# A selective-scan and ternary-FFN kernel: the input term of the scan made by TensorE for five of 16 pairs of states, and states handled in pairs

## The chip, the cores and the metric

One core of one Trainium2 chip runs the whole program. The metric is the device time of one launch in microseconds (us). The kernel before takes 226.84 us, the median of 3 runs (226.61 to 227.04). Engines are called by their names here: TensorE (PE in the profile), VectorE (DVE), ScalarE (ACT), GpSimd (POOL) and SyncE (SP), which issues nearly all the transfers.

## The reference, cut to what matters

Four sequences of 256 tokens, 256 channels. A state-space layer (16 states per channel) is gated by the normalised x and added to x; then comes a feed-forward block with ternary weights and 8-bit activations.

```python
x = x + ssm(ctx, layernorm(x))            # layer 1
x = x + ffn(layernorm(x))                 # layer 2

def ssm(h, z):                            # h (4,256,128), z (4,256,256)
    u = silu(depthwise_conv4(in_proj_w @ h) + conv_b)          # 256 channels x 256 steps
    dt_lo, B, C = split(x_proj_w @ u, [8, 16, 16])
    delta = softplus(dt_proj_w @ dt_lo + dt_proj_b)
    for t: state = state * exp(delta[t] * A) + delta[t]*u[t]*B[t]   # 16 states per channel
           y[t] = sum_n state[n] * C[t, n]
    return (y + D * u) * silu(z)

def bit_linear(x, w, b):                  # x in 127 steps of its token's maximum
    return round(x*127/gx)*gx/127 @ clip(round(w/gw), -1, 1)*gw + b
def ffn(x): return bit_linear(silu(bit_linear(x, gate)) * bit_linear(x, val), out)
```

## The kernel before, in words

**Tiling.** The four sequences go in two groups `g` of two (`BG`); channels lie on the 128 partitions in two halves `eh`. A row of work is 128 partitions x 512 (two sequences of 256 steps, one half of the channels, one state). So a group has 16 states x 2 halves = 32 units, and the kernel has 64 units in all, taken in order of the state, `eh` the inner loop.

**One unit of the scan.** ScalarE writes the decay exp(delta*A) into one of three PSUM banks (`decays`, line 653). GpSimd writes the drive, du*B, for both halves of one state at once, 128x1024, from `du` and from `b_wide`, the rows of B that a transfer has copied onto all partitions (`scan_drive`, lines 489 and 491). VectorE runs the scan (`scan`, line 898): one input is the decay in PSUM, the other the drive in SBUF. The state is then multiplied ("weighed") by C. For 22 of the 32 states VectorE does it, 128x512 each (line 908), with C spread over the partitions in the PSUM bank `cwide` by a TensorE product of a selector and C cut in three bf16 parts (`spread_c`, line 1177). For the ten states in `POOL_C` GpSimd does it, 128x1024 (line 501), with C loaded onto all partitions by a transfer. TensorE adds the weighed rows, transposed, into `ysum` (line 1156).

**What sets the order.** Nothing reorders instructions: each engine runs its own list, which the loops over the 64 units write out, and the engines wait for each other by semaphores. All other work is hung between the units by tables of unit numbers at the head of the file (`PE_Z`, `DVE_SPLIT`, `POOL_SOFTPLUS`, ...): group 1's convolution, projections and softplus, the rounding and turning of the ternary weights, and from unit 33 on the gate and the feed-forward block of group 0. Group 1's feed-forward block comes after the last unit, with nothing beside it.

**Around it.** VectorE makes the statistics of x before the first unit (line 816) and normalises x in eight steps beside the first units (line 825), it splits C (lines 865 to 871), ends the softplus (lines 877 to 889) and clips the ternary weights (line 945). GpSimd makes D*u (line 435), powers for the norms (line 443), group 1's softplus in part (lines 461 to 469), adds x (line 509), the parts of the token scales (lines 520 to 536) and adds the output bias to the residual (line 549).

Of the kernel before, what the change touches and what calls it, by code (L numbers as in the profile page):

```python
# [16 lines left out]
F32 = mybir.dt.float32  # L20
# [35 lines left out]
PE_Z, ACT_Z = (10, 11, 34, 36), (37, 38)  # L56
PE_PROJ, ACT_U, ACT_PROJ = 11, 14, 14
PE_PRE, ACT_PRE = (13, 14), (16, 18)
POOL_SOFTPLUS = (10, 11, 12, 13)
DVE_SPLIT, DVE_DELTA = 14, 27  # L60
ACT_WSUM, PE_WSUM, DVE_WSUM = (0, 2, 6), 11, 14
ACT_ROUND = (19, 21, 26)
PE_ROWS = (21, 26, 27, 28, 30, 31)
ACT_ROWS = (25, 28, 31, 32, 33, 35)
DVE_CLIP = (32, 34, 39)
DVE_GATED, DVE_STATS, DVE_INPUT = 33, 35, 37
POOL_SKIP, POOL_X1, POOL_RSTD, POOL_X1B = 9, 18, 19, 21
ACT_RND, POOL_PARTS = 40, 20
PE_COLS, ACT_COLS = 38, 41
PE_GATE, ACT_GATE = (39, 44, 51, 53), (44, 47, 56, 58)  # L70
PE_VAL, DVE_VAL, DVE_VAL2 = (45, 48, 59, 60), (46, 48, 60, 62), (47, 49, 61, 62)
ACT_QUANT, PE_TURN, ACT_TURN = (52, 54, 65, 68), (49, 54, 65), (53, 61, 67)
PE_OUT, DVE_OUT = (50, 58, 67), (51, 60)
POOL_C = (2, 5, 8, 13, 17, 19, 21, 24, 26, 28)
POOL_WAIT, SUM_WAIT = 3, 6
TURNS, WARM = (6, 6), (20, 3)


def on_pool(i):

    return i // EH in POOL_C


def rank(i):

    return sum(on_pool(k) == on_pool(i) for k in range(i))


def sums_at(j):

    return [i for i in range(max(0, j - SUM_WAIT), j)
            if 0 <= i < G * UNITS and j - (i - i % EH if on_pool(i) else i) == (SUM_WAIT if on_pool(i) else 2)]


SUMS = [i for j in range(G * UNITS + SUM_WAIT + 1) for i in sums_at(j)]


def work_tiles():

    first = ["inp", "ctx0", "conv0", "xin", "xproj", "dtw", "xc00", "conv1", "proj0", "pre00", "pre01", "ctx1"]
    scans = ["xc10", "xc11", "z0", "z1", "proj1", "wsum", "pre10", "pre11"]
    scans += [f"w{m}{k}" for m in "gvo" for k in range(4)] + ["z2", "z3"]
# [35 lines left out]
def block_program(nc, x, ctx, in_proj_w, conv_w, conv_b, x_proj_w, dt_proj_w, dt_proj_b, A_log, D,  # L142
# [3 lines left out]
    with stack:  # L146
# [6 lines left out]
        def sem(name):  # L153
# [59 lines left out]
        wrec = sb("wrec", [P, 4])  # L213
        ternary = sb("ternary", [P, 3, HT * DI], BF16)
# [7 lines left out]
        x1 = xhat[:, 0:GT]  # L222
        hn = xhat[:, GT:2 * GT]
# [18 lines left out]
        yflat = ysum[:].rearrange("p t e -> p (t e)")  # L242
        banks = [work[0][:], work[1][:], yflat[:, 0:BANK], yflat[:, BANK:2 * BANK],
                 *(d[:] for d in decay), cwide[:]]
        bc_rows = nc.dram_tensor("bc_rows", (G * 2 * NS, W), F32, kind="Internal").ap()
# [11 lines left out]
        s_ident, s_const = sem("ident_ready"), sem("constants_ready")  # L257
# [3 lines left out]
        s_xhat = sem("xhat_ready")  # L261
        s_cparts = sem("cparts_ready")
        s_expln = sem("exp_and_ln_ready")
        s_du = sem("du_ready")
        s_skip = sem("skip_ready")
        s_decay = sem("decay_ready")
        s_forget = sem("first_decays_zero")
        s_sel = sem("selector_ready")
        s_bstored = sem("b_and_c_rows_stored")
        s_cload = [sem(f"c_loaded{i}") for i in range(2)]  # L270
        s_poolw = sem("pool_wstate_ready")
# [1124 lines left out]
```

## Time and profile before

| | |
|---|---|
| median of 3 runs | 226.84 us (226.61 to 227.04) |
| span of the profiled execution | 224.8 us |
| what the median has over the span | 2.0 us |
| first unit's scan starts | 26.94 us |
| last weighing ends | 186.84 us |
| from there to the end | 37.96 us |
| VectorE busy over the span | 83% |
| PE, ScalarE, GpSimd busy | 67%, 58%, 61% |

The profiled execution is known by its span; the time of a run is what the table's first row gives, and the 2.0 us between them lie before the first and after the last instruction. The profile gives busy time per engine, groups of instructions by line, the instructions of an engine in order of time, and the chain of waits that ended last. A group of instructions is one line of the kernel; "out<-in" are the program's names of the tiles.

### The profile page before, as it was taken

Reading aid. Unit: us, or ns where it says so; the run is one execution under the profiler, and the core shown is the slowest. Engines: PE = TensorE matmul, PEld = TensorE weight load, DVE = VectorE, ACT = ScalarE, POOL = GpSimd, SP = SyncE. Lnnn points to the kernel's source line nnn. Section 1 sums busy time; section 2 is a strip of 40 time slices with the busy share of each in tenths; the row PEclk is TensorE's granted clock in tenths of the full one; section 3 lists DMA queues with packets and bytes.
Section 4 is the critical chain, followed back from the end, with each engine's and each line's share of the span. In section 5 each row is a group of like instructions: output and inputs, shape, how many; then the busy total and the mean of one; then the engine's idle time right before and its main releaser. Section 6 shows DMA issues by size and latency. Waiting matters only on the chain.

```text
span 224.8 us, 2405 instructions
## 1 busy us (share of the span) xinstructions
PE 150.9 (67%) x706; PEld 92.9 (41%) x706; DVE 186.5 (83%) x284; ACT 129.3 (58%) x197; POOL 136.8 (61%) x132
## 2 busy tenths in 40 slices
PE   6983088643979197059630777926986667899983
PEld 5531054232636186048620533504435265334552
DVE  3789999998089999999999968797869998838661
ACT  2578675336585996076341758736498015376772
POOL 5036499778900999896685999999139202691000
PEclk9995559978585769758785596985589969999999
DMA  4894943261400223004003304314000000000002
GB/s 107 231 343 123 339 146 112 87 189 42 140 13 0 75 66 92 4 0 141 0 0 98 135 3 136 73 71 140 23 1 3 23 0 0 0 28 0 23 23 70
DMA packets 12689, 17.44 MB, mean 78 GB/s; under 512 B 3468, under 2 KB 9012, under 8 KB 12678
## 3 DMA queue, kind: packets, MB, share of 16 engines
q1 hardware_dynamic: 12678, 17.30, 24.5%
q8 instruction: 5, 0.08, 0.2%
q14 instruction: 6, 0.05, 0.1%
HBM read 16.11 MB, written 1.19 MB: 77 GB/s over the span
## 4 chain that ended last, share of the span: by engine, by line
DVE 19%; PE 16%; ACT 9%; issue 6%; POOL 5%; DVEq 0%; POOLq 0%; ACTq 0%
DVE wstate L908 3%; PE work L1242 2%; DVE state L898 2%; PE work L1282 2%; DVE gam L981 2%; DVE xhat L825 2%; PE decay L1067 2%; ACT decay L653 2%; DVE pool_state L898 2%; DVE wstage L976 2%; POOL drive L491 2%; ACT gT L722 2%; ACT wstage L703 1%; PE decay L1242 1%; PE work L1249 1%
## 5 line engine op out<-in xcount | busy, mean ns | idle before, releaser
L491 POOL TENSOR_TENSOR drive<-du,b_wide 128x1024 f32<-128x1024 f32 x31 | 74.2, 2407 | 2.9 <-DVE state L898 1.8
L653 ACT ACTIVATE decay<-delta,aneg 128x510 f32<-128x510 f32 x64 | 42.9, 684 | 45.9 <-DVE state L898 23.3
L898 DVE TENSOR_TENSOR_SCAN state<-decay,drive 128x512 f32<-128x512 f32 x44 | 52.4, 1208 | 0.9 <-issue 0.9
L1156 PE MATMUL ysum<-ident,wstate 128*128 128x128 f32 x176 | 32.9, 332 | 10.6 <-DVE wstate L908 10.6
L908 DVE TENSOR_TENSOR wstate<-state,cwide 128x512 f32<-128x512 f32 x44 | 29.1, 663 | 12.2 <-issue 11.8
L1156 PEld LDWEIGHTS ysum<-ident,wstate 128*128 128x128 f32 x176 | 26.1, 172 | 18.8 <-DVE wstate L908 13.8
L501 POOL TENSOR_TENSOR pool_wstate<-pool_state,c_wide 128x1024 f32<-128x1024 f32 x10 | 23.7, 2367 | 11.4 <-PE ysum L1156 8.6
L898 DVE TENSOR_TENSOR_SCAN pool_state<-decay,drive 128x512 f32<-128x512 f32 x20 | 24.3, 1214 | 0.2 <-ACT decay L653 0.2
L1067 PE MATMUL work<-ident,wstage 128*128 128x128 f32 x80 | 14.2, 331 | 11.4 <-ACT ternary L677 7.7
L1177 PE MATMUL cwide<-cparts,sel 128*128 128x512 bf16 x22 | 10.6, 483 | 15.4 <-DVE wstate L908 14.2
L1067 PEld LDWEIGHTS work<-ident,wstage 128*128 128x128 f32 x80 | 11.8, 174 | 12.7 <-ACT ternary L677 8.1
L1242 PE MATMUL work<-ternary,qT 128*128 128x512 bf16 x46 | 16.3, 445 | 1.1 <-DVE wstage L976 0.8
L1156 PE MATMUL ysum<-ident,pool_wstate 128*128 128x128 f32 x80 | 13.3, 322 | 1.6 <-POOL pool_wstate L501 1.6
L716 ACT ACTIVATE wstage<-wstage,gam 128x512 f32<-128x512 f32 x16 | 10.6, 716 | 6.0 <-DVE gam L984 6.0
L509 POOL TENSOR_TENSOR xhat<-xhat,x_in 128x1024 f32<-128x1024 f32 (+1 forms) x2 | 3.6, 1814 | 16.0 <-DVE xhat L926 12.5
L1156 PEld LDWEIGHTS ysum<-ident,pool_wstate 128*128 128x128 f32 x80 | 11.9, 171 | 2.7 <-POOL pool_wstate L501 1.9
L976 DVE SCALAR_TENSOR_TENSOR wstage<-work,gam,wstage 128x512 f32<-128x512 f32 x12 | 8.7, 744 | 4.8 <-ACT wstage L703 3.4
L1067 PE MATMUL work<-ident,xhat 128*128 128x128 f32 x24 | 6.2, 420 | 9.6 <-ACT xhat L689 5.9
L1177 PEld LDWEIGHTS cwide<-cparts,sel 128*128 128x128 bf16 x22 | 2.5, 112 | 20.4 <-DVE wstate L908 17.6
L1156 PE MATMUL ysum<-ident,skip 128*128 128x128 f32 x16 | 3.0, 352 | 10.7 <-issue 8.7
L981 DVE TENSOR_REDUCE gam<-wstage 128x1 f32<-128x1024 f32 x8 | 9.8, 1220 | 0.3
L1249 PE MATMUL work<-bias_rows,acol 9*128 9x512 bf16 x23 | 9.8, 432 | 0.0
(180 smaller groups left out, 298.7 us busy)
## 6 DMA issues: line engine op xcount, KB each, us to landing
b_wide<-bc_rows SPq DMA_DIRECT2D x16, 512.0 KB, 4.5
c_wide<-bc_rows SPq DMA_DIRECT2D x10, 256.0 KB, 3.5
x_in<-in_x SPq DMA_DIRECT2D x2, 512.0 KB, 4.9
wstage<-in_L_ffn_gate_w SPq DMA_DIRECT2D x1, 1024.0 KB, 7.8
wstage<-in_L_ffn_val_w SPq DMA_DIRECT2D x1, 1024.0 KB, 10.3
wstage<-in_L_ffn_out_w SPq DMA_DIRECT2D x1, 1024.0 KB, 9.0
ctx_in<-in_ctx SPq DMA_DIRECT2D x2, 256.0 KB, 4.4
out<-wtap SPq DMA_DIRECT2D x4, 128.0 KB, 1.7
```

The lines of the kernel that those rows point to most:

```text
L491: nc.gpsimd.tensor_tensor(drive[:, m % NDR], du[:, m // NS], rows.unsqueeze(1).to_broadcast([P, EH, W]), ALU.mult).then_inc(s_drive, 1)
L501: nc.gpsimd.tensor_tensor(pool_wstate[:], pool_state[:, k % NPS], c_wide[:, k % 2].unsqueeze(1).to_broadcast([P, EH, W]), ALU.mult).then_i ...
L653: nc.scalar.activation(v[:, :, 1:L], d[:, :, 1:L], ACT.Exp, scale=aneg[:, eh, n:n + 1]).then_inc(s_decay, 1)
L898: nc.vector.tensor_tensor_scan(dst, decay[i % ND][:], drive[:, i // EH % NDR, i % EH], 0.0, ALU.mult, ALU.add).then_inc(s_scan, 1)
L908: nc.vector.tensor_tensor(wstate[:, rank(i) % NWS], state[:, rank(i) % NST], cwide[:], ALU.mult).then_inc(s_wst, 1)
L976: release(nc.vector.scalar_tensor_tensor(v, bank[:], gam[:, 3, t:t + 1], v, ALU.mult, ALU.mult), name)
L981: link(nc.vector.tensor_reduce(gam[:, 5, t:t + 1], gv[:, t], axis=AX.X, op=ALU.max, apply_absolute_value=True))
L1067: return nc.tensor.matmul(dst, lhsT=src, rhs=ident[0:src.shape[0], 0:src.shape[0]], start=True, stop=True, is_transpose=True, **flags)
L1156: last = nc.tensor.matmul(ysum[:, k, eh * P:(eh + 1) * P], lhsT=src[:, k * P:(k + 1) * P], rhs=ident[:], start=start and k % LB == 0, stop ...
L1177: nc.tensor.matmul(cwide[:], lhsT=sel[:, m % NS], rhs=cparts[:, m // NS], start=True, stop=True).then_inc(s_cwide, 1)
L1242: nc.tensor.matmul(bank[:], lhsT=qT[:, d, t * P:(t + 1) * P], rhs=wT[:, d, cols], start=d == 0, stop=False)
L1249: fill(nc.tensor.matmul(banks[TILE[name][0]], lhsT=acol[rows, t * P:(t + 1) * P], rhs=bias_rows[rows, cols], start=False, stop=True), name)
```

## The change

The loop goes over pairs of states. A slot is (pair of states, half of the channels, group): 32 slots, each 128x1024, of two units, one for each sequence. A scan is still 128x512, now one sequence with two states side by side.

- **Drive.** For five of the 16 pairs (`DIAG_PAIRS`; ten slots) GpSimd spreads B's columns on the diagonals of 128x128 matrices, one 128x1024 instruction a pair (`diagonals`), and TensorE multiplies the turned du by them into PSUM (`drives`, two products of 256 columns in float32 for a unit). For the other 11 pairs (22 slots) GpSimd multiplies du by B's rows on all partitions, 128x1024 (`drive_slot`), into `pool_drive` in SBUF.
- **Decay.** It lies in SBUF in place of PSUM, for all slots.
- **Weighing.** C is loaded onto all partitions for every pair; `cwide`, the selector and the split of C go. GpSimd weighs 22 slots (`weigh`), VectorE the ten in `DVE_SLOTS`, each in one 128x1024 instruction whose two inputs are both in SBUF.
- **Head.** dt_proj_w times x_proj_w's first rows is formed once (`wd`), so that the softplus doesn't wait for the projection; delta of the later halves is summed by TensorE (`add_delta`). The statistics of x move from ahead of the first unit to units 2 to 5. D*u becomes a TensorE product with a diagonal.
- **Others.** silu of the normalised x is one ScalarE instruction per tile (`silu_x`) in place of VectorE's normalising; the ternary weights come from ScalarE's Sign in place of copy and clip; VectorE adds x; two small instructions fewer per scale.

```diff
-NDR = 4
-ND = 3
-NPS = 2
-NB = 2
...
-POOL_C = (2, 5, 8, 13, 17, 19, 21, 24, 26, 28)
...
+ORDER = [(0, 0), (1, 0), (0, 1), (1, 1)] + [(p, eh) for p in range(2, NP) for eh in range(EH)]
...
+ND = 4
+NDRV = 4
+NST = 3
+NPW = 2
+NDG = 2
+NCW = 3
+NBW = 2
+NPD = 2
+DIAG_PAIRS = (0, 1, NP, NP + 2, NP + 4)
+DVE_SLOTS = (4, 6, 11, 13, 15, 17, 19, 21, 23, NSLOT - 1)
+POOL_LEAD = 2
...
-        decay = [pb(f"decay{i}", [P, BANK]) for i in range(ND)]
-        cwide = pb("cwide", [P, BANK])
+        decay = sb("decay", [P, ND, BG, 2, L])
+        pool_drive = sb("pool_drive", [P, NPD, BG, 2, L])
+        drive = [pb(f"drive{i}", [P, BANK]) for i in range(NDRV)]
...
+            def drive_slot(s):
+                g, p, eh = slot_parts(s)
+                k, r = g * NP + p, drive_rank(s)
+                w = wide_rank(k)
+                if r >= NPD:
+                    pool.wait_ge(s_scan, BG * [j for j in range(s) if not on_diag(j)][r - NPD] + BG)
...
+                rows = du[:, g, eh].rearrange("p (b l) -> p b l", b=BG).unsqueeze(2).to_broadcast([P, BG, 2, L])
+                nc.gpsimd.tensor_tensor(pool_drive[:, r % NPD], rows, b_wide[:, w % NBW], ALU.mult).then_inc(s_pdrive, 1)
...
+            for s in range(NSLOT):
+                for k in DIAG_PAIRS[2:]:
+                    if s == slots_of(k)[0] - DIAG_LEAD:
+                        diagonals(k)
+                if s + POOL_LEAD < NSLOT and not on_diag(s + POOL_LEAD):
+                    drive_slot(s + POOL_LEAD)
+                if s not in DVE_SLOTS:
+                    weigh(s)
+                if s == POOL_XRSTD:
+                    rstd(0)
...
             def scan(i):
-                nc.vector.tensor_tensor_scan(dst, decay[i % ND][:], drive[:, i // EH % NDR, i % EH], 0.0,
-                                             ALU.mult, ALU.add).then_inc(s_scan, 1)
+                s, b = divmod(i, BG)
...
+                if on_diag(s):
+                    dve.wait_ge(s_drive, BG * r + b + 1)
+                    rows = drive[(BG * r + b) % NDRV][:]
+                else:
+                    dve.wait_ge(s_pdrive, r + 1)
+                    rows = pool_drive[:, r % NPD, b].rearrange("p n l -> p (n l)")
+                if s >= NST and b == 0:
+                    wait_weighed(dve, s - NST)
+                nc.vector.tensor_tensor_scan(state[:, s % NST, b].rearrange("p n l -> p (n l)"),
+                                             decay[:, s % ND, b].rearrange("p n l -> p (n l)"), rows, 0.0,
+                                             ALU.mult, ALU.add).then_inc(s_scan, 1)
...
-                nc.vector.tensor_tensor(wstate[:, rank(i) % NWS], state[:, rank(i) % NST], cwide[:],
+                nc.vector.tensor_tensor(flat(wstate[:]), flat(state[:, s % NST]), flat(c_wide[:, k % NCW]),
                                         ALU.mult).then_inc(s_wst, 1)
...
+                for c in range(LB):
+                    t = b * LB + c
+                    last = nc.tensor.matmul(bank[:, :, c * P:(c + 1) * P], lhsT=duT[:, g, t, eh], rhs=bdiag[:, d % NDG, t],
+                                            start=True, stop=True)
```

On GpSimd, in the middle of group 0, the list before has a drive for every state (both halves) and here and there a weighing and a part of group 1's softplus:

```order
L491 TENSOR_TENSOR drive<-du,b_wide 128x1024
L461 TENSOR_SCALAR du<-mag 128x1024
L491 TENSOR_TENSOR drive<-du,b_wide 128x1024
L501 TENSOR_TENSOR pool_wstate<-pool_state,c_wide 128x1024
L465 TENSOR_SCALAR du<-du 128x1024
L491 TENSOR_TENSOR drive<-du,b_wide 128x1024
L467 TENSOR_TENSOR du<-du,mag 128x1024
```

After the change the same place of GpSimd's list (slots 2 to 8; 520 is the drive of the slot two ahead, 532 the weighing) is, following the power for x's norm:

```order
L483 TENSOR_SCALAR nv<-nv 128x8
L520 TENSOR_TENSOR pool_drive<-du,b_wide 128x1024
L532 TENSOR_TENSOR pool_wstate<-state,c_wide 128x1024
L520 TENSOR_TENSOR pool_drive<-du,b_wide 128x1024
L532 TENSOR_TENSOR pool_wstate<-state,c_wide 128x1024
L520 TENSOR_TENSOR pool_drive<-du,b_wide 128x1024 x2
L532 TENSOR_TENSOR pool_wstate<-state,c_wide 128x1024
L520 TENSOR_TENSOR pool_drive<-du,b_wide 128x1024 x2
```

The softplus has gone, and weighings stand between most of the drives; the power for the norm of x, which waits for VectorE's statistics, stands ahead of the first of these drives.

On VectorE, before, in the same part of group 0, scans (898) with a PSUM decay alternate with weighings of 512 (908):

```order
L898 SCALAR_TENSOR_TENSOR pool_state<-decay,drive 128x512
L908 TENSOR_TENSOR wstate<-state,cwide 128x512
L898 SCALAR_TENSOR_TENSOR pool_state<-decay,drive 128x512
L898 SCALAR_TENSOR_TENSOR state<-decay,drive 128x512 x2
L908 TENSOR_TENSOR wstate<-state,cwide 128x512
L898 SCALAR_TENSOR_TENSOR state<-decay,drive 128x512
L908 TENSOR_TENSOR wstate<-state,cwide 128x512
L935 TENSOR_SCALAR wgam<-work 128x3
```

After it, VectorE's list from the last statistics of x on, slots 3 to 6 (970 is the scan, `drive` in PSUM by TensorE, `pool_drive` in SBUF by GpSimd):

```order
L880 BN_STATS stats<-x_in 128x6 x2
L883 BN_AGGR mv<-stats 128x2 x2
L970 SCALAR_TENSOR_TENSOR state<-decay,drive 128x512 x2
L970 SCALAR_TENSOR_TENSOR state<-decay,pool_drive 128x512 x2
L983 TENSOR_TENSOR wstate<-state,c_wide 128x1024
L970 SCALAR_TENSOR_TENSOR state<-decay,pool_drive 128x512 x3
L1009 TENSOR_SCALAR wgam<-work 128x3
```

Most weighings have left VectorE's list, and from slot 4 on its scans read `pool_drive` and `decay`, both in SBUF.

## Rows read from the trace of the kernel before

**Rows 1.** The page's busy times: us, share of the span, instructions.

```profile
PE 150.9 (67%) x706; PEld 92.9 (41%) x706; DVE 186.5 (83%) x284; ACT 129.3 (58%) x197; POOL 136.8 (61%) x132
```

**Rows 2.** Three stretches: units of group 0, of group 1, the rest; busy us.

```profile
core 0: us, PE busy (x) PEld busy (x) DVE busy (x) ACT busy (x) POOL busy (x), PEclk, DMA share, GB/s
26.94:106.50 79.56, 51.57 (x230) 36.59 (x230) 71.52 (x80) 48.83 (x69) 61.69 (x29) 0.74 0.26 84
106.50:186.84 80.34, 51.27 (x241) 30.79 (x241) 70.34 (x100) 41.66 (x62) 54.10 (x40) 0.77 0.15 49
186.84:224.80 37.96, 31.97 (x185) 16.76 (x183) 24.02 (x57) 22.61 (x39) 11.07 (x37) 1.00 0.06 21
```

**Rows 3.** The page's groups: busy, mean ns of one, idle time before and its releaser.

```profile
L898 DVE TENSOR_TENSOR_SCAN state<-decay,drive 128x512 f32<-128x512 f32 x44 | 52.4, 1208 | 0.9 <-issue 0.9
L908 DVE TENSOR_TENSOR wstate<-state,cwide 128x512 f32<-128x512 f32 x44 | 29.1, 663 | 12.2 <-issue 11.8
L501 POOL TENSOR_TENSOR pool_wstate<-pool_state,c_wide 128x1024 f32<-128x1024 f32 x10 | 23.7, 2367 | 11.4 <-PE ysum L1156 8.6
```

**Rows 4.** Line 898's instructions: duration ns min/median/max.

```profile
L898 DVE TENSOR_TENSOR_SCAN state<-decay,drive x44: 1191/1210/1224, 26.9 to 184.4; 128x512 f32<-128x512 f32 x44
L898 DVE TENSOR_TENSOR_SCAN pool_state<-decay,drive x20: 1206/1216/1224, 37.8 to 167.9; 128x512 f32<-128x512 f32 x20
```

**Rows 5.** VectorE in order of time: start us, duration us.

```profile
21.41 0.69 DVE L882 TENSOR_TENSOR delta<-du,lnw 128x512 f32<-128x512 f32 x1
22.75 0.42 DVE L877 TENSOR_SCALAR du<-mag 128x512 f32<-128x512 f32 x1
23.93 1.65 DVE L880 TENSOR_TENSOR du<-pre,du 128x512 f32<-128x512 f32 x1
...
35.33 2.56 DVE L825 TENSOR_SCALAR xhat<-x_in,mv,nv 128x256 f32<-128x256 f32 x1
37.81 1.21 DVE L898 TENSOR_TENSOR_SCAN pool_state<-decay,drive 128x512 f32<-128x512 f32 x1
38.94 0.66 DVE L908 TENSOR_TENSOR wstate<-state,cwide 128x512 f32<-128x512 f32 x1
...
41.30 0.39 DVE L825 TENSOR_SCALAR xhat<-x_in,mv,nv 128x256 f32<-128x256 f32 x1
...
89.59 2.77 DVE L888 TENSOR_TENSOR delta<-du,lnw 128x1024 f32<-128x1024 f32 x1
92.47 3.17 DVE L889 TENSOR_TENSOR du<-delta,u 128x1024 f32<-128x1024 f32 x1
```

**Rows 6.** GpSimd in order of time, the same columns.

```profile
23.75 1.27 POOL L489 TENSOR_TENSOR drive<-du,b_wide 128x512 f32<-128x512 f32 x1 [3.05 <-DMA b_wide<-bc_rows]
28.33 9.41 POOL L491 TENSOR_TENSOR drive<-du,b_wide 128x1024 f32<-128x1024 f32 x4
...
88.94 5.62 POOL L491 TENSOR_TENSOR drive<-du,b_wide 128x1024 f32<-128x1024 f32 x2
95.72 2.34 POOL L491 TENSOR_TENSOR drive<-du,b_wide 128x1024 f32<-128x1024 f32 x1 [1.16 <-DVE du L889]
```

**Rows 7.** Groups with shapes kept apart, VectorE and GpSimd.

```profile
L816 DVE BATCH_NORM_STATS2 stats<-x_in 128x6 f32<-128x256 f32 x8 | 2.7, 410 | 0.0
L921 DVE TENSOR_TENSOR xhat<-ysum,szT 128x1024 f32<-128x1024 f32 x1 | 1.2, 1211 | 0.0
L418 POOL TENSOR_SCALAR_AFFINE_SELECT ident<-ident 128x128 f32<-128x128 f32 x1 | 0.3, 292 | 0.2 <-POOL ident L417 0.2
L443 POOL TENSOR_TENSOR nv<-nv,half 128x8 f32<-128x8 f32 x1 | 1.7, 1654 | 0.1
L549 POOL TENSOR_TENSOR x_in<-xhat,obias 128x256 f32<-128x256 f32 x4 | 2.8, 722 | 0.0
```

**Rows 8.** The page's transfers: KB each, median us from issue to landing.

```profile
b_wide<-bc_rows SPq DMA_DIRECT2D x16, 512.0 KB, 4.5
```

**Rows 9.** The chain of waits: start us, us, what.

```profile
123.10 0.52 POOL gam L520 x2
...
126.44 0.19 POOL apart L533
```

More of the change, by code:

```diff
@@ L89, in sums_at @@
[L89 to L95, printed above, removed]
+NP = NS // 2
+SLOTS = NP * EH
+UNITS = SLOTS * BG
+ORDER = [(0, 0), (1, 0), (0, 1), (1, 1)] + [(p, eh) for p in range(2, NP) for eh in range(EH)]
+NSLOT = G * SLOTS
+NUNIT = G * UNITS
+ND = 4
[5 more added lines that the diff above has]
+NBW = 2
@@ new lines, with slot_of, slot_parts, slots_of @@
+TURNS, WARM = (6, 6), (16, 3)
+def slot_of(g, p, eh):
+    return g * SLOTS + ORDER.index((p, eh))
+def slot_parts(s):
+    g, k = divmod(s, SLOTS)
+    p, eh = ORDER[k]
+    return g, p, eh
+def slots_of(k):
+    return sorted(slot_of(k // NP, k % NP, eh) for eh in range(EH))
+def pair_of(s):
+    g, p, _ = slot_parts(s)
+    return g * NP + p
+def on_diag(s):
+    return pair_of(s) in DIAG_PAIRS
+def drive_rank(s):
+    return sum(on_diag(k) == on_diag(s) for k in range(s))
+def wide_rank(k):
+    return sum(j not in DIAG_PAIRS for j in range(k))
@@ L237, in block_program @@
         work = [pb(f"work{i}", [P, BANK]) for i in range(2)]
[L238 to L239 removed]
         ysum = pb("ysum", [P, GT, DI])
[L242 to L245, printed above, removed]
+        drive = [pb(f"drive{i}", [P, BANK]) for i in range(NDRV)]
+        banks = [work[0][:], work[1][:], *(ysum[:, LB * b:LB * (b + 1)].rearrange("p t e -> p (t e)") for b in range(BG)),
+                 *(d[:] for d in drive)]
+        DRIVE0 = 4
+        bc_rows = nc.dram_tensor("bc_rows", (G, 2, NP, BG, 2, L), F32, kind="Internal").ap()
         bias_split = nc.dram_tensor("bias_split", (2, PARTS, HID), BF16, kind="Internal").ap()
@@ L762, in _ @@
+                if t == ACT_RND:
+                    for k in range(GT):
+                        ffn_round(0, k)
+                if t == ACT_COLS:
                     ffn_half(0, 0)
@@ new lines, in sums @@
+            def sums(s):
+                _, _, eh = slot_parts(s)
+                wait_weighed(pe, s)
+                src = wstate[:] if s in DVE_SLOTS else pool_wstate[:, pool_rank(s) % NPW]
+                for n in range(2):
+                    for t in range(GT):
+                        b, c = divmod(t, LB)
+                        last = nc.tensor.matmul(ysum[:, t, eh * P:(eh + 1) * P], lhsT=src[:, b, n, c * P:(c + 1) * P],
+                                                rhs=ident[:], start=False, stop=True, is_transpose=True,
+                                                skip_group_check=True)
+                last.then_inc(s_ysum, 1)
@@ L1340, in _ @@
                     ffn_products(0, PE_VAL.index(i), "val")
-            wait_weighed(pe, G * UNITS - 1)
+            for s in range((PE_OUT[-1] - SUM_LAG) // BG + 1, NSLOT):
+                sums(s)
             warm(WARM[0])
```

975 lines of the change are left out of this document (505 added, 470 removed).

## The prediction

> **What bounds the kernel now.** I read the busy times first [rows 1], then the same by stretches [rows 2], then the groups [rows 3], then VectorE and GpSimd side by side in order of time [rows 5, 6]. The reader is to see that VectorE is busy in 71.5 of 79.6 us of group 0's units and in 70.3 of 80.3 us of group 1's. The 64 scans and 44 weighings make 52.4 + 24.3 + 29.1 = 106 us of it (24.3 is 20 scans at the 1216 ns of [rows 4]). GpSimd is busy in 61.7 and 54.1 us of these stretches, so it has 44 us of slack. The rest, 37.96 us, is group 1's feed-forward block, which the change leaves nearly as it is.
>
> The second thing to see is that VectorE and GpSimd shut each other out. Line 889, 128x1024 with both inputs in SBUF, takes 3.17 us and line 888 2.77 us, where line 921, as large but with one input in PSUM, takes 1.21 [rows 5, 7]. Beside them GpSimd's two drives take 5.62 us, where four in a row take 9.41, 2.35 each [rows 6]: 0.9 us lost. The times fit turns: line 888 waits for the first drive, runs, the second drive runs while line 889 waits, and the next drive starts at 95.72, just after 889 ends at 95.64. Line 880 is the same on a small scale: it starts at 23.93 inside a GpSimd drive (23.75 to 25.02) and takes 1.65 us, where line 882, the same shape, takes 0.69 [rows 5, 6]. Line 825, SBUF to SBUF, takes 0.39 or 2.56 us [rows 5]. The scans never do this: 64 of them lie between 1191 and 1224 ns [rows 4], and each has its decay in PSUM.
>
> [...]
>
> **What the change does to that.** The scans of the 22 slots that GpSimd drives now read `decay` and `pool_drive`, both in SBUF. That is 44 of the 64 scans. The ten VectorE weighings also have two SBUF inputs. So I ask what must take turns from the first GpSimd drive on.
>
> *Head.* Before, the first scan starts at 26.94. The split of C and the statistics leave VectorE's path, TensorE gets more to do (the product of the two projections, turning B and du, summing delta, three drives), and all that ends, by my count of the same steps at about 0.7 us an operation of 512 [rows 5], near 25.7; bounds 24 and 28. Then come slots 0 to 3, driven from PSUM. VectorE runs six scans at 1.13 (from 37.81 to 38.94 in [rows 5]), one copy of 0.6 and the statistics of x (eight at 0.41 [rows 7] and eight small ones, 3.8 with the waits between them): 25.7 + 6.8 + 0.6 + 3.8 = 36.9. GpSimd stands at the power for x's norm until then, since it comes behind the weighing of slot 1; 1.65 us [rows 7] and three small ones make 2.5. Its first drive, slot 4's, starts near 39.4, and behind it wait slot 4's scan and the weighing of slot 2.
>
> *GpSimd from 39.4 on.* 22 drives at 2.35 = 51.7 [rows 6]. 20 weighings (22 less slots 0 and 1) at 2.35 (alone 2367 ns [rows 3]) = 47.0. Three diagonals: no row has this size; the nearest is line 418, 292 ns for 128 columns [rows 7], which by its slope would be about 1.05 for 1024, and the other bound is 2.35, a product of that size; I take 1.05, since it is the same operation: 3.2. A power 1.2, the scale parts 3.5 (123.10 to 126.63 [rows 9]), four additions at 0.72 = 2.9 [rows 7]. Sum 109.5 us.
>
> *VectorE's part that must take turns with it.* 44 scans at 1.13 = 49.7; ten weighings, bounded by 1.13 (line 921's 1.21 less the overlap) without a wait and 3.17 with one, where the excess is GpSimd's time and is counted already: 11.3. Softplus bits of group 1 2.2 (0.42 and 0.69 twice [rows 5]), two additions of x 1.4, four normalisings at 0.39 = 1.6 [rows 5]. Sum 66.2 us.
>
> *The ledger.* 39.4 + 109.5 + 66.2 = 215.1. Other work of VectorE (20 scans from PSUM, of which eight are before 39.4, the feed-forward block's pieces of group 0) lies beside GpSimd's instructions and costs nothing. GpSimd also waits for VectorE's statistics ahead of the second power and for the token scales ahead of the parts, where nothing of either holds the port: 3 us, from nothing to 6. Last weighing at 218.1, against 186.84 before. The tail stays 38.0: the last weighing is 1024 and not 512 (+0.6), a small instruction less in each scale (0.15 each) gives it back. Span 256.1, and with the 2.0 us around the span **258 us**. Less than 247 would need the turns to be worth 10 us less than counted (GpSimd not holding the port in its first and last tenths of a us, 86 turns at 0.1); more than 270 would need 0.1 us lost at each hand-over.
>
> *What goes to nothing.* The 29.1 us of VectorE weighings, C's split, the clipping and the normalising leave VectorE, and that is worth nothing here, since VectorE then waits for the port. The transfers grow to 16 of C and 11 of B at 512 KB, 27 x 4.5 = 122 us [rows 8] in some 180, loaded two slots ahead or more: hidden. TensorE has 51.6 + 51.3 = 103 us of work in 160 [rows 2]; 17 late drives at about 1 us, the sums of delta and the turns of du add some 28, and `cwide` leaves: hidden in 190 us. If the port does not bind, both covers get thin.
>
> **The rivals.** (1) *The scans don't take turns*, only the weighings and small ones do. For it: no row shows a scan with two SBUF inputs, and a scan takes 1.13 us for 512 where a weighing takes 0.58 (its 0.66 less the overlap), so it reads at half the rate. Against it: lines 880, 888, 889 have nothing in common but their two inputs in SBUF. Then GpSimd has 109.5 + 16.5 of turns (11.3 + 2.2 + 1.4 + 1.6) = 126. VectorE has 56 scans, 63.3, the ten weighings 11.3, some 25 of feed-forward pieces, gate, statistics and softplus, and some 18 waits of half a GpSimd instruction, 21: 121. Two engines so near each other lose a few us to each other's waits: 39.4 + 130 = 169.4, and with 38 and 2.0 **210 us**, faster by 17; bounds 200 (VectorE's waits hidden) and 222 (TensorE, 131 us of work in 130, late with its sums). It decides from the point where the 49.7 us of the scans are less than a third on the path.
>
> (2) *Turns in part.* The scans exclude GpSimd, but GpSimd's idle places fit them, as a scan slips between two waits. Then a third to two thirds of the 49.7 is hidden: about 235 us, 226 to 246. For it: GpSimd waits on semaphores before each instruction. Against it: with drives two slots ahead both engines always have the next instruction ready.
>
> (3) *The start slips.* C's first rows land late and the first weighing with them: the rows are stored near 19, read back by 23, landed 4.5 us later near 28 [rows 8], and slot 0's weighing is due at 28. It is slower in any case, by at most 3 us, and is in the ranges.
>
> **How the numbers follow.** Turns for the scans 0.55, no turns 0.37, in part 0.08. The prediction is the likeliest, 258, with its own range 247 to 270. The range of 8 in 10 must reach into the second case: 205 to 268 leaves out a quarter of that case below and a tenth of the first above. What a measurement of this kernel can tell from no change is 0.2%, 0.45 us. Faster is the second case and a little of the third: 0.38; within 0.2%: 0.02; slower: 0.60.
>
> **What would show each step.** The scans of `pool_drive`: durations between 1.2 and 3.6 us by turns, against 1.2 for those of `drive`; GpSimd's drives and weighings 2.35 to 4.7. If both stay at 1.2 and 2.35 the first case is wrong and the time is near 210. GpSimd's first drive near 39.4 behind the power; VectorE's weighing of 1024 between 1.2 and 3.6; the last weighing near 218; GpSimd with hardly an idle us between 40 and 218 save before the second power. It is wrong also if GpSimd's power does not hold up its first drive.

## The result, and the profile after

| | before | after |
|---|---|---|
| median | 226.94 us (226.61 to 228.97) | **269.45 us** (268.78 to 271.34) |
| profiled execution | 226.84 us, span 224.8 | 271.34 us, span 269.3 |

The ratio is 1.187, with a 95% interval of 1.181 to 1.193: the change costs 42.6 us. It is slower, as forecast, and 11.5 us slower than the forecast of 258. That lies inside the likeliest case's own range (247 to 270) and 1.5 us above the range on record (205 to 268). The spans of the other three runs are 266.8 to 267.9, so the profiled one is about 2 us longer than the typical run. Those three have no profile; the profiled one has a head 3 us longer than most profiled variants, as shown below. For the variants with 8 and 16 pairs and a single buffer two of the four executions were 2 to 3% longer at a lower granted clock, and the times below are the means of the two others (258.8 and 232.2 us; the medians of all four, which later expectations quote, are 261.53 and 234.63).

The busy times of the page after, to be set against [rows 1]:

```profile
PE 183.8 (68%) x824; PEld 118.2 (44%) x830; DVE 209.4 (78%) x222; ACT 132.6 (49%) x205; POOL 157.9 (59%) x129
```

VectorE has 62 instructions fewer and is busy for 23 us more. The groups of the page say where that sits (busy us, mean ns of one, idle time before it and its releaser); they answer to [rows 3]:

```profile
L970 DVE TENSOR_TENSOR_SCAN state<-decay,pool_drive 128x512 f32<-128x512 f32 x44 | 95.1, 2196 | 6.6 <-issue 6.4
L520 POOL TENSOR_TENSOR pool_drive<-du,b_wide 128x1024 f32<-128x1024 f32 x22 | 65.3, 2968 | 16.5 <-DVE state L970 16.5
L532 POOL TENSOR_TENSOR pool_wstate<-state,c_wide 128x1024 f32<-128x1024 f32 x22 | 60.8, 2762 | 23.9 <-DVE state L970 21.0
...
L983 DVE TENSOR_TENSOR wstate<-state,c_wide 128x1024 f32<-128x1024 f32 x10 | 22.8, 2279 | 4.7 <-PE ysum L1264 4.4
L970 DVE TENSOR_TENSOR_SCAN state<-decay,drive 128x512 f32<-128x512 f32 x20 | 23.3, 1200 | 1.8 <-PE drive L1252 1.8
...
L505 POOL TENSOR_SCALAR_AFFINE_SELECT bdiag<-bt 128x1024 f32<-128x1024 f32 x5 | 7.3, 1472 | 15.6 <-ACT bt L659 15.6
```

One line of the program, 970, gives two groups. The 44 scans whose drive lies in SBUF take 2.20 us each, the 20 whose drive lies in PSUM 1.20. By single instructions (duration ns min/median/max, first and last start), to be set against [rows 4]:

```profile
L970 DVE TENSOR_TENSOR_SCAN state<-decay,pool_drive x44: 1191/1998/3383, 47.4 to 227.4; 128x512 f32<-128x512 f32 x44
L970 DVE TENSOR_TENSOR_SCAN state<-decay,drive x20: 1185/1196/1221, 31.3 to 186.0; 128x512 f32<-128x512 f32 x20
```

The longest is longer than the shortest by 2.19 us, nearly one whole GpSimd product (2.35 us where it runs alone). VectorE and GpSimd in order of time, start and duration in us, show the turns, where [rows 5, 6] show none for scans:

```profile
47.45 6.51 DVE L970 TENSOR_TENSOR_SCAN state<-decay,pool_drive 128x512 f32<-128x512 f32 x2 [2.82 <-issue]
53.99 3.18 DVE L983 TENSOR_TENSOR wstate<-state,c_wide 128x1024 f32<-128x1024 f32 x1
57.10 5.61 DVE L970 TENSOR_TENSOR_SCAN state<-decay,pool_drive 128x512 f32<-128x512 f32 x3
```

```profile
44.99 2.37 POOL L520 TENSOR_TENSOR pool_drive<-du,b_wide 128x1024 f32<-128x1024 f32 x1
47.33 2.33 POOL L532 TENSOR_TENSOR pool_wstate<-state,c_wide 128x1024 f32<-128x1024 f32 x1
49.63 3.25 POOL L520 TENSOR_TENSOR pool_drive<-du,b_wide 128x1024 f32<-128x1024 f32 x1
52.84 3.25 POOL L532 TENSOR_TENSOR pool_wstate<-state,c_wide 128x1024 f32<-128x1024 f32 x1
56.05 3.35 POOL L520 TENSOR_TENSOR pool_drive<-du,b_wide 128x1024 f32<-128x1024 f32 x1
61.67 3.19 POOL L520 TENSOR_TENSOR pool_drive<-du,b_wide 128x1024 f32<-128x1024 f32 x1 [2.28 <-DVE state L970]
```

The first two GpSimd products have the port nearly to themselves; from 49.6 to 60 us each step of either engine takes 3.2 to 3.4 us, one of each. The program by stretches (head from the first scan to GpSimd's first drive, the units in two halves, the tail), against [rows 2]:

```profile
core 0: us, PE busy (x) PEld busy (x) DVE busy (x) ACT busy (x) POOL busy (x), PEclk, DMA share, GB/s
31.30:45.00 13.70, 13.39 (x64) 9.67 (x63) 13.18 (x25) 10.57 (x16) 6.99 (x7) 1.00 0.60 211
45.00:130.00 85.00, 50.47 (x212) 33.82 (x211) 79.24 (x41) 45.37 (x67) 69.47 (x24) 0.74 0.22 79
130.00:229.90 99.90, 63.54 (x304) 44.41 (x306) 80.89 (x81) 43.08 (x64) 65.34 (x42) 0.74 0.15 53
229.90:269.30 39.40, 30.57 (x169) 16.22 (x170) 23.11 (x52) 18.84 (x35) 10.27 (x36) 0.96 0.06 21
```

The tail is 39.4 us against 38.0. The rest of the loss is in the head and above all in the units, where TensorE is idle for 36 to 41% of the time. The chain that ended last, by engine:

```profile
PE 29%; issue 23%; DVE 21%; POOL 19%; ACT 5%; DMA 1%; DVEq 0%; ACTq 0%; POOLq 0%; SPq 0%
```

### The profile page after: what moved, and what is told of

The parts are those of the page before. It is cut to its first block, busy times and chain, and to the rows that moved or that the text cites. A ratio compares the mean times of both kernels' runs of the same rounds, so it can differ in the third digit from the quotient of the medians.

```text
span 269.3 us, 2612 instructions
## 1 busy us (share of the span) xinstructions
PE 183.8 (68%) x824; PEld 118.2 (44%) x830; DVE 209.4 (78%) x222; ACT 132.6 (49%) x205; POOL 157.9 (59%) x129
## 3 DMA queue, kind: packets, MB, share of 16 engines
HBM read 19.25 MB, written 1.19 MB: 76 GB/s over the span
## 4 chain that ended last, share of the span: by engine, by line
PE 29%; issue 23%; DVE 21%; POOL 19%; ACT 5%; DMA 1%; DVEq 0%; ACTq 0%; POOLq 0%; SPq 0%
POOL pool_drive L520 10%; DVE state L970 8%; POOL pool_wstate L532 5%; PE ysum L1264 4%; PE work L1136 3%; PE drive L1136 3%; PE drive L1252 2%; PE work L1371 2%; DVE stats L880 2%; PE work L1328 2%; DVE mag L890 2%; PE drive L1328 2%; POOL bdiag L505 2%; DVE wstage L1039 2%; PE ysum L1232 1%
## 5 line engine op out<-in xcount | busy, mean ns | idle before, releaser
L970 DVE TENSOR_TENSOR_SCAN state<-decay,pool_drive 128x512 f32<-128x512 f32 x44 | 95.1, 2196 | 6.6 <-issue 6.4
L520 POOL TENSOR_TENSOR pool_drive<-du,b_wide 128x1024 f32<-128x1024 f32 x22 | 65.3, 2968 | 16.5 <-DVE state L970 16.5
L532 POOL TENSOR_TENSOR pool_wstate<-state,c_wide 128x1024 f32<-128x1024 f32 x22 | 60.8, 2762 | 23.9 <-DVE state L970 21.0
L1252 PE MATMUL drive<-bdiag,duT 128*128 128x256 f32 x80 | 22.8, 417 | 18.0 <-POOL bdiag L505 18.0
L1264 PE MATMUL ysum<-ident,pool_wstate 128*128 128x128 f32 x176 | 30.7, 332 | 3.0 <-POOL pool_wstate L532 3.0
L983 DVE TENSOR_TENSOR wstate<-state,c_wide 128x1024 f32<-128x1024 f32 x10 | 22.8, 2279 | 4.7 <-PE ysum L1264 4.4
L1252 PEld LDWEIGHTS drive<-bdiag,duT 128*128 128x128 f32 x80 | 15.6, 209 | 22.5 <-issue 19.1
L970 DVE TENSOR_TENSOR_SCAN state<-decay,drive 128x512 f32<-128x512 f32 x20 | 23.3, 1200 | 1.8 <-PE drive L1252 1.8
L1136 PEld LDWEIGHTS work<-ident,wstage 128*128 128x128 f32 x80 | 13.2, 194 | 21.1 <-ACT ternary L719 10.1
L476 POOL TENSOR_SCALAR nv<-mv 128x2 f32<-128x2 f32 (+2 forms) x4 | 1.2, 297 | 22.7 <-DVE mv L883 22.7
L1264 PE MATMUL ysum<-ident,wstate 128*128 128x128 f32 x80 | 11.6, 293 | 0.0
L1264 PEld LDWEIGHTS ysum<-ident,wstate 128*128 128x128 f32 x80 | 10.3, 155 | 1.2 <-issue 1.0
```

The source lines that it names most:

```text
L520: nc.gpsimd.tensor_tensor(pool_drive[:, r % NPD], rows, b_wide[:, w % NBW], ALU.mult).then_inc(s_pdrive, 1)
L532: nc.gpsimd.tensor_tensor(flat(pool_wstate[:, r % NPW]), flat(state[:, s % NST]), flat(c_wide[:, k % NCW]), ALU.mult).then_inc(s_poolw, 1)
L970: nc.vector.tensor_tensor_scan(state[:, s % NST, b].rearrange("p n l -> p (n l)"), decay[:, s % ND, b].rearrange("p n l -> p (n l)"), rows ...
L983: nc.vector.tensor_tensor(flat(wstate[:]), flat(state[:, s % NST]), flat(c_wide[:, k % NCW]), ALU.mult).then_inc(s_wst, 1)
L1136: return nc.tensor.matmul(dst, lhsT=src, rhs=ident[0:src.shape[0], 0:src.shape[0]], start=True, stop=True, is_transpose=True, **flags)
L1252: last = nc.tensor.matmul(bank[:, :, c * P:(c + 1) * P], lhsT=duT[:, g, t, eh], rhs=bdiag[:, d % NDG, t], start=True, stop=True)
```

## The experiments

Theory 1: a scan that reads decay and drive from SBUF takes turns with GpSimd. Theory 2, the main rival: it does not, and the time went into longer waits of another kind (the single buffer of VectorE's weighings, the power, GpSimd's order). Unless said otherwise every time below is the median, and every ratio is to the kernel before, run on the same chip (about 226.8 us). In the code cuts `...` stands for lines left out.

**One cause, put into the kernel before.** Its decays go to SBUF, so all 64 scans have two SBUF inputs and nothing else of the change is there. Two things come with it: ScalarE writes SBUF in place of PSUM, and `gT` shares the bytes of `pre`.

```
+        decay_sb = sb("decay_sb", [P, ND, W])
...
-                v = decay[i % ND][:].rearrange("p (b l) -> p b l", b=BG)
+                v = decay_sb[:, i % ND].rearrange("p (b l) -> p b l", b=BG)
...
-                nc.vector.tensor_tensor_scan(dst, decay[i % ND][:], drive[:, i // EH % NDR, i % EH], 0.0,
+                nc.vector.tensor_tensor_scan(dst, decay_sb[:, i % ND], drive[:, i // EH % NDR, i % EH], 0.0,
```

> The kernel before with one thing changed: the decays lie in SBUF, so that all 64 scans have two SBUF inputs (gT shares the bytes of pre to make room). Theory 1, turns: a scan with two SBUF inputs and a GpSimd product shut each other out. GpSimd is busy 116 us in the 160 us of units and the scans add 64 x 1.13 = 72, so the units end near 26.9 + 188 = 215 and the time is near 255 (245 to 262); scans between 1.2 and 3.6 us, GpSimd's drives up to 3.4. Theory 2, the coarse coupling of the slots is what costs: nothing changes, 227. Theory 3, reading SBUF makes a scan itself slower: scans longer but all alike, GpSimd's drives stay at 2.36.

Measured: 280.39 us, ratio 1.241 (1.232 to 1.249): 53.6 us slower. Scans of line 899 and drives of line 492 in that kernel, by single instructions:

```profile
L899 DVE TENSOR_TENSOR_SCAN state<-decay_sb,drive x44: 1191/2180/3355, 27.0 to 237.8; 128x512 f32<-128x512 f32 x44
L492 POOL TENSOR_TENSOR drive<-du,b_wide x31: 2340/3252/3287, 29.3 to 218.6; 128x1024 f32<-128x1024 f32 x31
```

```profile
L909 DVE TENSOR_TENSOR wstate<-state,cwide x44: 652/656/687, 32.6 to 239.5; 128x512 f32<-128x512 f32 x44
```

In the same kernel the weighings of 512, which read `cwide` in PSUM, stay at 0.66 us. The shortest scans still take 1.19 us, so theory 3 (a slower scan by itself) falls, theory 1 holds in kind, and theory 2 falls as the main cause. My size for it (255) was too small by 25: I had added up only what holds the port, that is, what must take turns. VectorE, busy for 240.6 us of 278.9, does much else between two scans, and GpSimd can use that time only where it doesn't wait for VectorE. The waits of this profile charge GpSimd with 18.3 us for scans, 15.0 for statistics and 22.7 for the gated rows; which of these make up the 25 I didn't separate.

**The cause taken out of the kernel after.** The 44 scans read a fourth, constant PSUM bank in place of `pool_drive`. GpSimd still makes its drives, and every wait on them stays; du*B is left out of the states of 22 slots. TensorE's drives have three banks in place of four, so what is left over may hold a little of that.

```
-NDRV = 4
+NDRV = 3
...
-                    rows = pool_drive[:, r % NPD, b].rearrange("p n l -> p (n l)")
+                    rows = drive[3][:]
```

> The changed kernel, where the scans of the 22 slots that GpSimd drives still wait for pool_drive but read a fixed PSUM bank in its place, so the product du*B is left out of these states; TensorE's drives get three banks and not four. Theory 1, turns: 44 scans fall out of the ledger, 49.7 us at most, and VectorE and GpSimd are then near 120 to 126 us each from 45 on: time 215 to 232, these scans at 1.2 us and GpSimd's products at 2.35 save beside weighings. Theory 2, coarse coupling: 260 or more. Theory 3, the decay's place in SBUF makes it slow: 265 or more.

Measured: 241.28 us, ratio 1.070 (1.063 to 1.077): 28.2 us of the 42.6 are gone.

```profile
L970 DVE TENSOR_TENSOR_SCAN state<-decay,drive x64: 1186/1206/1221, 28.4 to 197.4; 128x512 f32<-128x512 f32 x64
```

```profile
L520 POOL TENSOR_TENSOR pool_drive<-du,b_wide x22: 2342/2357/3305, 42.1 to 187.8; 128x1024 f32<-128x1024 f32 x22
```

All 64 scans take 1.2 us and GpSimd's drives 2.36. Still it comes neither to 210 nor into the 215 to 232 expected, and stays slower than before. What is late next stands in its waits (engine, line, waited for: us in all, times, longest):

```profile
DVE wstate L983 <- PE ysum L1264: 15.2, 5, 5.9
DVE wtap L1053 <- PE work L1371: 7.7, 1, 7.7
DVE du L953 <- PE work L1212: 7.4, 2, 5.9
```

VectorE's weighing waits for TensorE to have summed the one before, because `wstate` has a single buffer, and the scans wait behind it. This edit gives it a second one (`gT` then shares the bytes of `relu`):

```
-        wstate = sb("wstate", [P, BG, 2, L])
+        wstate = sb("wstate", [P, 2, BG, 2, L])
...
-                if dve_rank(s):
-                    dve.wait_ge(s_ysum, DVE_SLOTS[dve_rank(s) - 1] + 1)
+                if dve_rank(s) > 1:
+                    dve.wait_ge(s_ysum, DVE_SLOTS[dve_rank(s) - 2] + 1)
```

> As the run in which the scans read a fixed PSUM bank (du*B left out of the states of 22 slots; 241.3 us), and VectorE's weighed rows have two buffers in place of one. There VectorE waited 15.2 us for TensorE's sums ahead of five weighings. Theory 2 (what is left above the kernel before is the coarse coupling, one buffer and lists in order): 8 to 15 us faster, 226 to 233. Theory 4 (the wait only changes its name, since TensorE's sums themselves wait for GpSimd's weighings): 238 to 241.

Measured: 232.95 us, ratio 1.026 (1.017 to 1.036), 8.3 less. The same edit in the kernel after, with its turns:

> The changed kernel with two buffers for VectorE's weighed rows and nothing else. There VectorE waits for the sums only 4.4 us ahead of two weighings. Theory 1, the turns bind where GpSimd drives: 0 to 4 us faster, 265 to 269. Theory 2, the single buffer binds whether or not there are turns: 10 us faster or more.

Measured: 262.7 us, ratio 1.158 (1.149 to 1.166): 6.8 less, between my two ranges, though the page charged VectorE's weighings with only 4.4 us of this wait. Part of the rest is what it had delayed behind it: GpSimd's wait for the statistics of the second power (in the rows further below) goes from 9.26 to 6.86 us. A part may be the head, where the two profiles differ by 2.9 us. With two buffers the exclusion of the scans alone costs 262.7 − 232.95 = 29.8 us.

**More diagonals, fewer turns.** With TensorE driving more pairs fewer scans read `pool_drive`, and GpSimd exchanges two drives of a pair (4.7 us) for one affine select (1.09 us). The wait for a free `bdiag` has to name the slot.

```
-DIAG_PAIRS = (0, 1, NP, NP + 2, NP + 4)
+DIAG_PAIRS = (0, 1, 3, 5, NP, NP + 2, NP + 4, NP + 6)
...
-                    pool.wait_ge(s_drive, BG * EH * (r - NDG + 1))
+                    pool.wait_ge(s_drive, BG * (drive_rank(slots_of(DIAG_PAIRS[r - NDG])[-1]) + 1))
```

> The changed kernel with eight pairs by TensorE in place of five. Theory 1, turns: each of the six slots that move takes a drive of 2.35 and two scans of 1.13 out of the ledger, 27.7 in all, and three diagonals put 3.2 in: 24 us faster, 245 (240 to 252). Theory 2, coarse coupling: GpSimd saves 11 and its diagonals cost 3, 8 us faster or less, 261 to 269.

> All 16 pairs by TensorE: no scan has two SBUF inputs. Theory 1, turns: 101 us leave the ledger and 11.6 come in, so it binds no longer; TensorE gets 88 products more, about 37 us on 184, and binds: 225 to 240. Theory 2, coarse coupling: the slots are as coarse as before, 255 or more.

Measured: 258.8 us (1.146, 1.135 to 1.158) with 8 pairs, and 232.2 (1.028, 1.019 to 1.038) with 16, `tuple(range(G * NP))`. The first missed my 245 widely: 32 scans still take 2.07 us at the median. With 16 pairs the scans are all at 1.2, and the single buffer is what is late:

```profile
DVE wstate L983 <- PE ysum L1264: 25.0, 7, 6.8
```

So the series was run again with two buffers: 8, 12 and 16 pairs.

> Eight pairs by TensorE (261.5 us) with two buffers. The three pairs more were worth 8 us and not the 24 of the ledger. Theory 5, both limits stand in a row (as turns go, the single buffer comes next): 245 to 252. Theory 1 alone or another wait: 258 to 262.

> Twelve pairs by TensorE, four by GpSimd, with two buffers. Beside 16 pairs (217.4 us) TensorE is rid of 32 products of 0.4 us, 12 us, and GpSimd gets 8 drives and 16 scans take turns. Theory 6, TensorE is the bound at 16 pairs: a little faster, 211 to 217. Theory 1, the turns cost more than TensorE saves: 8 x 2.35 + 16 x 1.13 = 37 us more on the port, less 4 diagonals, 218 to 232.

> All 16 pairs by TensorE (234.6 us) with two buffers for VectorE's weighed rows. VectorE waited 25.0 us for the sums ahead of seven weighings. Theory 2: 5 to 12 us faster, 223 to 230. Theory 4, TensorE is the bound there (busy 85%): 232 to 235.

| pairs by TensorE | scans that take turns | us (95% of the ratio) | granted TensorE clock |
|---|---|---|---|
| 5 | 44 | 262.7 (1.149 to 1.166) | 0.82 |
| 8 | 32 | 256.25 (1.121 to 1.136) | 0.87 |
| 12 | 16 | 231.45 (1.011 to 1.028) | 0.93 |
| 16 | 0 | **217.44** (0.950 to 0.968) | 0.98 |

The last one beats both kernels: 4.1% faster than before, and below my 223 to 230. Eight pairs came between my two ranges, twelve into the one of theory 1. With a single buffer 16 pairs took 232.2, so there the second buffer is worth 15 us; with 8 pairs it is worth 3, no more than two heads differ by (below). The rows of the last one:

```profile
PE 189.4 (88%) x999; PEld 130.9 (61%) x1006; DVE 156.6 (73%) x222; ACT 132.5 (62%) x205; POOL 95.8 (45%) x118
```

```profile
L970 DVE TENSOR_TENSOR_SCAN state<-decay,drive x64: 1186/1206/1221, 28.4 to 173.2; 128x512 f32<-128x512 f32 x64
L983 DVE TENSOR_TENSOR wstate<-state,c_wide x10: 1225/1252/2689, 45.7 to 174.4; 128x1024 f32<-128x1024 f32 x10
```

```profile
PE 66%; DVE 21%; issue 5%; ACT 4%; DMA 2%; ACTq 0%; DVEq 0%; SPq 0%
```

The last row is the chain by engine: TensorE holds 66% of it, and 29% in the kernel after. The bound has moved. GpSimd, busy for 95.8 us, is far from it. The steps of the series aren't even (−6.4, −24.8, −14.0 us for 12, 16 and 16 scans less), and each step also takes drives from GpSimd and changes TensorE's clock, so I read no price of one scan from it.

**Who weighs.** Seven weighings more go from GpSimd to VectorE, with two buffers:

```
-DVE_SLOTS = (4, 6, 11, 13, 15, 17, 19, 21, 23, NSLOT - 1)
+DVE_SLOTS = (4, 5, 6, 7, 8, 9, 10, 11, 12, 13, 14, 15, 17, 19, 21, 23, NSLOT - 1)
```

> The changed kernel with VectorE weighing all 12 slots of group 0 from slot 4 on (17 in all, not ten), with two buffers. Theory 1, the ledger of turns: a weighing holds the port 1.13 us on VectorE and 2.35 on GpSimd, so seven moved are worth 8.5 us: 261 (258 to 264). Theory 2: GpSimd's list gets shorter and VectorE's longer; 265 to 270.

Measured: 265.9 us, ratio 1.173 (1.163 to 1.182). Against two buffers alone (262.7) the seven are worth nothing; the 3 us the wrong way may be the head, since the profile of this run has the first scan at 31.4 and the other at 28.4. My ledger had given each 1.2 us (2.35 less 1.13 of port time).

**The power for x's norm.** `POOL_XRSTD` goes from 1 to 4, so that GpSimd's first drives don't wait for VectorE's statistics.

> The changed kernel with GpSimd's power for x's norm behind slot 4 in place of slot 1. The first GpSimd drive can start after the weighing of slot 1 near 40 in place of 45. Theory 1 with the start in the ledger: 4 to 5 us faster, 265. Theory 4, the drive then waits for b_wide or the scans of slots 2 and 3 run into it: under 2 us.

Measured: 271.11 us, ratio 1.192 (1.182 to 1.202), no change. In GpSimd's order of time the first drive is early, and what follows it waits instead; the power itself is slower, since it now runs beside VectorE's scans (2.50 us against 1.67):

```profile
37.16 2.37 POOL L520 TENSOR_TENSOR pool_drive<-du,b_wide 128x1024 f32<-128x1024 f32 x1
42.22 3.02 POOL L532 TENSOR_TENSOR pool_wstate<-state,c_wide 128x1024 f32<-128x1024 f32 x1 [2.70 <-PE ysum L1264]
...
56.13 2.50 POOL L477 TENSOR_TENSOR nv<-nv,half 128x8 f32<-128x8 f32 x1
```

**A part of the change that helps.** The kernel before with Sign in place of the clipping on VectorE, and with the scales' factors fused:

```
-                release(nc.scalar.activation(dst, t[:], ACT.Copy, bias=-MAGIC), name)
+                release(nc.scalar.activation(dst, t[:], ACT.Sign, bias=negmagic[:]), name)
...
-                if i in DVE_CLIP:
+                if False:
...
-                link(nc.vector.tensor_scalar(gam[:, src, t0:t1], gam[:, src, t0:t1], FLOOR, None, ALU.max))
+                link(nc.vector.tensor_scalar(gam[:, src, t0:t1], gam[:, src, t0:t1], FLOOR, 1.0 / QMAX, ALU.max, ALU.mult))
```

> The kernel before with two small parts of the change alone: the ternary weights by ScalarE's Sign (no clip on VectorE, 4.1 us) and one instruction less in each scale (0.15 us each, nine in group 1's tail and in the groups). VectorE is the bound of the units, so theory A: 3 to 5 us faster, 222 to 224. Theory B, the clips lie where VectorE waits for the feed-forward chain anyway: only the tail's scales count, 1 us, 225.8.

Measured: 222.3 us, ratio 0.980 (0.975 to 0.986): some 4 us faster in the kernel before, where VectorE is busy for 83% of the span.

## Why the prediction was right and where it was wrong

The mechanism was right and the sum was not: 269.45 us lies 1.5 us above the range on record. Two terms of the sum failed. The waits of GpSimd where nothing holds the port were put at "3 us, from nothing to 6", and the port is free for about 21 us; the work of TensorE ahead of the first scan was named and priced at nothing, and the head is 5.6 us late. The work on the port was counted too high by 11 us, which hid most of this. The upper end of the range failed too: the likeliest case reached to 270 by itself, and 268 was got by leaving a tenth of it out.

**The scans take turns: right.** This was the likeliest case, at 0.55, argued from lines 880, 888 and 889, none of them a scan. Of their signs one was misread in the prediction: the drive at 95.72 starts behind line 889 because it waits for the row that 889 writes ([rows 6]: 1.16 <-DVE du L889), not for the port; the long times of 888 and 889 stay. It is shown from both sides: alone it makes the kernel before 53.6 us slower, and without it the kernel after is 28.2 us faster. The Trainium skill ("SBUF — State Buffer", Who interferes with whom) states that a VectorE instruction with two SBUF inputs contends with a GpSimd instruction that reads SBUF, and doesn't name the scan. The trace agrees: 44 scans at 1.19 to 3.38 us with two SBUF inputs, 20 at 1.19 to 1.22 with one, in the same kernel.

The profiled span, 269.3, is 13.2 us over the 256.1 of the sum: 5.6 in the head, 6.2 in the units, 1.4 in the tail.

**The head: 5.6 us late.** I had the first scan at 25.7 and GpSimd's first drive at 39.4; they are at 31.30 and 45.00. The 13.7 us between the two are exactly as counted (six scans, a copy, the statistics, the power). The miss lies ahead of the first scan, in two waits of VectorE for TensorE:

```profile
28.83 0.69 DVE L953 TENSOR_TENSOR du<-work,u 128x512 f32<-128x512 f32 x1 [3.21 <-PE work L1212]
31.30 1.22 DVE L970 TENSOR_TENSOR_SCAN state<-decay,drive 128x512 f32<-128x512 f32 x1 [1.78 <-PE drive L1252]
```

The summing of delta and the first drives on TensorE were in my list and not priced. TensorE in order of time, first in this execution and then in the variant whose scans read PSUM, which has the same head:

```profile
24.72 1.91 PE L1208 MATMUL work<-relu,ident 128*128 128x512 f32 x2
26.43 1.51 PE L1210 MATMUL work<-lnw,ident 128*128 128x512 f32 x2
27.77 1.02 PE L1212 MATMUL work<-du,nident 128*128 128x512 f32 x2
```

```profile
23.20 1.02 PE L1208 MATMUL work<-relu,ident 128*128 128x512 f32 x2
24.06 1.02 PE L1210 MATMUL work<-lnw,ident 128*128 128x512 f32 x2
24.92 1.02 PE L1212 MATMUL work<-du,nident 128*128 128x512 f32 x2
```

The same products take up to twice as long here: from 24 to 26 us the granted clock is 0.50, TensorE's lower level, and 1.00 in the other variant. That is not all of the 2.9 us between the two first scans. TensorE is 1.2 us later already at 22.47 (the turning of du, at 21.29 there), where the record shows a clock of 1.00 in both; the two products of line 1408 near 8.9 take 1.80 us here and 1.13 there, and why stays open. In seven of the ten profiled variants of the kernel after the first scan is at 28.4 to 28.9, in the other three at 31.3 to 31.5, as here. So some 3 us over my 25.7 stand in every one of these profiles, and some 3 more in those with the slower head. The profiled execution is the longest of the four.

**The power holds up the first drive: true, and worth nothing.** In the trace the drive at 44.99 comes straight behind it. But with it out of the way the time stays 271: what I called a link of the sum was a place where time waits that is waited for later anyway.

**The ledger of the port: two misses that nearly cancel.** From 45.0 to 229.85, 184.9 us, I had 175.7 of turns and 3 of waits. When I lay the intervals of all GpSimd instructions and of VectorE's with two SBUF inputs over each other, the port is in use for about 164 us and free for about 21. In use it is 11 less than counted; a pair of turns takes 3.25 us where I added 1.13 + 2.35 = 3.48, which is 10 us over 44 scans. (Lines 890 and 934, with one tile in SBUF as input, took turns too, 0.40 us alone and up to 2.50 beside GpSimd; with them the port is in use for 2 us more.) Free it is 18 more. The step that failed is "3 us, from nothing to 6". The price of the diagonals, 1.05 us, came true (1.09) by luck: one row, 292 ns for 128 columns, gives no slope, and in proportion it would be 2.34. GpSimd in order of time at the second power, and VectorE beside it:

```profile
138.87 2.36 POOL L532 TENSOR_TENSOR pool_wstate<-state,c_wide 128x1024 f32<-128x1024 f32 x1
150.49 0.20 POOL L476 TENSOR_SCALAR nv<-mv 128x4 f32<-128x4 f32 x1 [9.26 <-DVE mv L883]
```

```profile
143.66 1.22 DVE L970 TENSOR_TENSOR_SCAN state<-decay,pool_drive 128x512 f32<-128x512 f32 x1
147.31 1.23 DVE L983 TENSOR_TENSOR wstate<-state,c_wide 128x1024 f32<-128x1024 f32 x1 [2.43 <-PE ysum L1264]
148.45 0.75 DVE L880 BATCH_NORM_STATS2 stats<-lnw 128x6 f32<-128x256 f32 x2
```

GpSimd waits for statistics, these stand behind a weighing, and the weighing waits for a sum of TensorE: three engines one after another. This one wait is 9.26 us, where I had 3 for it and the token scales together; 2.4 of it is the weighing's wait, as the run with two buffers shows (6.86), and the rest VectorE's own list, in which a scan and the additions of x stand ahead of the statistics. The same of the whole kernel, among the waits of the profile after:

```profile
POOL nv L476 <- DVE mv L883: 22.7, 4, 10.5
POOL pool_wstate L532 <- DVE state L970: 21.0, 6, 7.8
...
POOL pool_drive L520 <- DVE state L970: 16.5, 8, 3.3
...
DVE wtap L1053 <- PE work L1371: 6.1, 2, 4.5
...
DVE wstate L983 <- PE ysum L1264: 4.4, 2, 2.4
DVE wstage L1039 <- PE work L1335: 4.0, 1, 4.0
```

My test "GpSimd with hardly an idle us between 40 and 218" is plainly false: it is idle for 50 of the 184.9 us. The sum came near the truth because both engines were never far from the port, and not because GpSimd always had its next instruction ready. As a price list the ledger fails: it made 255 of a kernel that took 280, 245 of one that took 259, and it gave a gain to seven weighings that brought none.

**The rival without turns, 210 us: mis-sized.** Its condition can be made, and gives 241, or 233 with two buffers. In the profile of the second (231.42 us, span 229.2) GpSimd's first drive is at 42.1 against 39.4, the last weighing ends 147.8 us later against 130, and the tail is 39.3 against 38. So 18 of the 22 us are in the units: two engines with 126 and 121 us of work did not lose "a few us to each other's waits". Nor was either of them faster than the kernel before: by these two runs my 0.38 for faster would have been wrong even if scans took no turns. Which of the many small waits make up the 18 I didn't separate; that stays open.

**Hidden work.** That VectorE's relief of 29.1 us of weighings is worth nothing here no run shows by itself; seven weighings put back on VectorE cost nothing that can be read, which fits. TensorE is busy for 114 of the 185 us, but its work is hidden only in part: its sums hold up VectorE's weighings (the 6.8 us of the second buffer), and in the head it is late by 3 us. Clipping and the scales are worth some 4 us in the kernel before; that they are worth nothing while the port binds, and what the normalising is worth, no run tested.

## What to carry to other kernels

Before moving a product to GpSimd, list for each VectorE instruction that will read its result how many of its inputs lie in SBUF; where that becomes two, a GpSimd instruction beside it costs a turn, and a scan with its decay and drive in SBUF went from 1.2 to 2.2 us. If two engines are near each other in a ledger, the sum of their work is a lower bound only: add what each waits for the other through single buffers and in-order lists, and look first at the buffer with one copy (here 7, 3, 8 and 15 us in four variants). Work moved to the engine with time to spare was worth it only when all of it went: with all 16 pairs on TensorE and a second buffer the kernel runs at 217.4 us.

## What the runs showed of the hardware

- A VectorE scan of 128x512 fp32 with both inputs in SBUF and a GpSimd product that reads SBUF exclude each other: the scan takes 1.19 us alone and up to 3.39 beside it, the product of 128x1024 2.35 and up to 3.41. With either input in PSUM the scan takes 1.19 to 1.22 in every run.
- Where both engines had a next instruction they alternated one by one, though a scan alone takes 1.2 us and a product 2.35 (in the kernel after from 49.6 to 60 us each step of either takes 3.2 to 3.4).
- A VectorE tensor_scalar from SBUF to SBUF took turns too, with one tile as its input: line 890 (128x256) 0.40 us alone and 2.42 beside a product, line 934 (128x512) 0.40 and 2.50.
- An affine select of 128x1024 on GpSimd takes 1.09 us, under half of a product of that size, and 2.08 when it loses a turn.
- The granted TensorE clock is 0.74 in both halves of the units after, a mix of its two levels (1.2 and 2.4 GHz), while TensorE waits again and again for GpSimd and VectorE; over the kernel with 16 pairs it is 0.98, nearly all of it at 2.4. So TensorE is busy for 189.4 us with 999 matmuls there, and for 183.8 with 824 in the kernel after: the added work cost it 5.6 us of busy time.
